# A projection in the place of a transposition at the crossing of the five-tile chunk, and four head groups per loop turn in a two-layer cross-attention kernel

## The chip, the cores and the metric

The kernel runs on one core of a Trainium2 chip. The metric is the device time of one execution in microseconds. All operands are float32 in memory. On TensorE the kernel multiplies in reduced formats, and it gets the accuracy back by splitting each operand into a high part and a low part (`_hi` and `_lo`), so that one exact product is made of three matmuls.

## The reference, cut to what matters

1024 query rows `x` of width 128 attend to 6404 context rows of width 128, with 16 heads of 64. A mixture-of-experts layer follows, then a second attention and a second mixture. In layer 0 queries and keys are RMS-normalized per head, and the 1024 latent rows are keys and values too:

```python
# layer 0 (xn, ln: layer norms of context and latents; rmsnorm per head of 64)
q = ln @ Wq;  kv = concat([xn @ Wkv, ln @ Wkv])        # 7428 keys
sim = (rmsnorm(q) * scale) @ rmsnorm(k).T
out = softmax(sim) @ v;  x = x + tanh(g) * (out @ Wout + bout)
# layer 1 (no norm of q and k, one extra null key and value): 6405 keys
out = softmax(scale * q @ k.T) @ v
x = x + tanh(g) * layernorm(out @ Wo)
```

## The kernel before, in words

**Groups, chunks, steps, pairs.** The 16 heads are worked off in 8 groups of 2 (`GH = 2`, `NG = 8`). The keys lie in tiles of 128: 59 in layer 0 and 51 in layer 1. `CHUNKS` cuts the tiles into ten chunks per layer. In layer 0 all chunks have 6 tiles, but for chunk 4, which has 5. A chunk is gone through twice: once for queries 0 to 511 (n = 0), then for queries 512 to 1023 (n = 1), the two query halves. A step is one tile of keys with one query half and both heads. A group has 118 steps in layer 0 and 102 in layer 1. The loops go by pairs of steps: pair i holds steps 2i and 2i+1. Chunk 4 of layer 0 is steps 48 to 57, so pairs 24 to 28. As it has an odd number of tiles, pair 26 holds its last step of the first half (52) and its first step of the second half (53). That is the crossing, `crossed` in the code.

**What an engine does in pair i.** TensorE (PE): the scores of steps 2i+2 and 2i+3 (`score`, line 1135, two `scores_ps` buffers in turn). Then, in odd pairs, `mix_last` (line 1143). Then the products of probabilities and values of steps 2i and 2i+1, from the high part (`mix_high`, line 1153) and the low part (`mix_low`, line 1160), which add up in `out_ps`. ScalarE (ACT): `exp` of steps 2i+2 and 2i+3 (line 659 in layer 0, two instructions for a step). VectorE (DVE): `p_low` of these steps (line 818: probabilities minus their high part), and after the last step of a half of a chunk `add_out` (lines 829, 831), which adds `out_ps` into `out_acc` and so frees `out_ps`. The first `mix_high` of the next half waits for it (`o_added`). At the crossing DVE's order is `p_low(54)`, `add_out` of step 52, `p_low(55)`.

**Items.** Keys and values of the next chunk are made two tiles at a time. Such an item k is a load and a turn. The load is `project_kv` on PE (line 1070, six matmuls into `proj_ps`), then on ACT `read_kv` (lines 628, 630, and the square of 634 in layer 0), then on DVE `v_low` (802, 804) and `k_var` (792, 795), and GpSimd (POOL) makes the reciprocal root (590). The turn is `transpose_k` on PE (1078, two transposes), then on ACT `k_high` (639) and `v_wide` (645), then on DVE `k_low` (810). There is one `proj_ps`, so `project_kv` of an item waits until `k_low` of the item before is done (`lo_done`), and `transpose_k` waits for `v_low` of its own item. Queries of the next group (`q_rows`, `q_cols`) and the output product (`final`) use `proj_ps` in between, at pairs that stay the same under the change. In pair 24 DVE also runs `bound_norm` (lines 871, 873, 881), between `p_low(51)` and that pair's items.

**Where an item stands.** `schedule(L)` (lines 166 to 205) writes the order by hand. It spreads the loads and turns of the next chunk evenly over the pairs of the present one, and puts each at the nearest slot: "s", "m" or "e". On PE "s" is ahead of the pair's products of values, "m" between them and "e" behind them. On ACT and DVE "s" is between the two steps of the pair, and "m" and "e" are both behind the second. So on ACT a load at "s" is read ahead of the pair's second `exp`. Every engine works strictly through its own list.

**The loop over groups.** On each engine `Fori(0, NG // 2)` holds the code of two groups (`g = two * 2 + odd`), so that a layer has four turns and three jumps back, behind groups 1, 3 and 5 (groups are counted from 0).

Of the kernel before, what the change touches and what calls it, by code (L numbers as in the profile page):

```python
# [40 lines left out]
GH = 2  # L41
NG = H // GH
CHUNKS = ((6, 6, 6, 6, 5, 6, 6, 6, 6, 6), (6, 6, 6, 5, 4, 4, 4, 4, 6, 6))
NB = 6
NPL = 4
VW = 36
# [119 lines left out]
def schedule(L):  # L166

    tiles = CHUNKS[L]
    first = [sum(tiles[:c]) for c in range(len(tiles))]
    steps = [(c, n, t) for c, m in enumerate(tiles) for n in range(2) for t in range(m)]  # L170
    item0 = [sum((m + 1) // 2 for m in tiles[:c]) for c in range(len(tiles) + 1)]
    slots = (("s", 0.2), ("m", 0.55), ("e", 1.0))
    turn, load = {}, {}
    for c, pairs in enumerate(tiles):
        n_items = (tiles[(c + 1) % len(tiles)] + 1) // 2
        for k in range(2 * n_items):
            at = (k + 1) * pairs / (2 * n_items)
            _, pair, slot = min((abs(p + x - at), p, s) for p in range(pairs) for s, x in slots)
            where = turn if k % 2 == 0 else load
            assert first[c] + pair not in where  # L180
            where[first[c] + pair] = (slot, item0[c + 1] + (k + 1) // 2)
    ends = {}
    for i, (c, n, t) in enumerate(steps):
        if t == tiles[c] - 1:
            ends.setdefault(i // 2, []).append((i, 2 * c + n))
    free = [p for p in sorted(load) if load[p][0] == "e" and turn.get(p - 1, " ")[0] == "e" and p - 1 not in ends]
    final = [p for p in free if p >= 5][:4]
    q_row = [p for p in free if p > final[-1]][:2]
    q_col = [p for p in free if p >= q_row[1] + 6][:2]
    events = {}  # L190
    for rank, slot in enumerate("sme"):
        for kind, table in (("turn", turn), ("load", load)):
            for pair, (at, k) in table.items():
                if at == slot:
                    events.setdefault(pair, []).append((rank, kind, k))
    return steps, item0, turn, load, {p: [("sme"[rank], kind, k) for rank, kind, k in sorted(e)] for p, e in events.items()}, ends, final, q_row, q_col


def attention_layer(nc, A, L, sem_, sb_, layer_norm, ln_stats, ln_apply, rstd, B):
# [6 lines left out]
    NT = REST + 1  # L206
    TL = CHUNKS[L]
    TM = max(TL) + max(TL) % 2
# [16 lines left out]
    with scope:  # L225
        def sb(name, shape, dt=F32, to=scope):
            return sb_("a%d_%s" % (L, name), shape, dt, to)
# [224 lines left out]
        vlast = sb("v_last", [P, 2, TM, GH, VW], F16)  # L452
        probs = sb("probs", [P, NB, NQ])
        plow = sb("probs_lo", [P, NPL, NQ], R32)
# [60 lines left out]
        def step_at(n2):  # L515
            return STEPS[n2 % NS] + (n2 % NS,)
# [12 lines left out]
        with nc.Block() as block:  # L529
            @block.sync  # L530
            def _(sp):
                def load_kv(r):
                    sp.dma_start(wkv_raw[:, :], A[NAME + "wkv_g"][bass.ds(r, 1), :, :].rearrange("a p n -> p (a n)")).then_inc(wkv_in, 16)

                def load_q(r):
                    sp.dma_start(wq_raw[:, :], A[NAME + "wq_g"][bass.ds(r, 1), :, :].rearrange("a p n -> p (a n)")).then_inc(wq_in, 16)

                def load_o(r):
                    sp.wait_ge(ql_done, 2 * r + 2)
                    sp.dma_start(wo_raw[:, :], A[NAME + "wo_g"][bass.ds(r, 1), :, :].rearrange("a p n -> p (a n)")).then_inc(wo_in, 16)  # L540
                    sp.dma_start(fin, A[NAME + "we_g"][bass.ds(r, 1), :, :].rearrange("a p n -> p (a n)")).then_inc(wo_in, 16)

                def load_den(r):
                    sp.wait_ge(o_added, 2 + r * NADD)
                    sp.dma_start(den_row.unsqueeze(0), oacc[P - 1:P, :, :]).then_inc(den_out, 16)
                    sp.wait_ge(den_out, 16 * (r + 1))
                    sp.dma_start(sums[:, 0, :], den_row.rearrange("h (p x) -> (h p) x", x=GH * NQ // P)).then_inc(sum_in, 16)
                    sp.wait_ge(den_rec, r + 1)
                    sp.dma_start(inv_row.rearrange("h (p x) -> (h p) x", x=GH * NQ // P), sums[:, 1, :]).then_inc(inv_out, 16)
                    sp.wait_ge(inv_out, 16 * (r + 1))  # L550
                    sp.wait_ge(c_ready, r + 1)
                    sp.dma_start(den[:, :, :], inv_row.partition_broadcast(P)).then_inc(den_in, 16)
                    sp.wait_ge(den_in, 16 * (r + 1))

                load_kv(0)
                load_q(0)
                with sp.Fori(0, NG // 2) as two:
                    for odd in range(2):
                        g = two * 2 + odd
                        load_o(g)  # L560
                        load_den(g)
                        sp.wait_ge(wkv_lo, g + 1)
                        load_kv(g + 1)
                        sp.wait_ge(wq_lo, g + 1)
                        load_q(g + 1)
                        if L == 1:
                            sp.wait_ge(v_ready, (g + 1) * NI)
                            r_ = CTX_REST
                            wide = [1, GH, P - 1]
                            sp.dma_start(v16[r_:r_ + 1, LASTP, T_LAST, :, 0:P - 1],  # L570
                                         null16[0:1, 0:P - 1].unsqueeze(1).broadcast_to(wide)).then_inc(null_in, 16)
                            sp.dma_start(v32[r_:r_ + 1, LASTP, T_LAST, :, 0:P - 1].bitcast(F32),
                                         null32[:, 0:P - 1].bitcast(F32).unsqueeze(1).broadcast_to(wide)).then_inc(null_in, 16)
                            for h in range(GH):
                                sp.dma_start(vlast[r_:r_ + 1, LASTP, T_LAST, h, 4:5], null16[0:1, P - 1:P]).then_inc(null_in, 16)
                load_o(NG)
                load_den(NG)

            @block.gpsimd
            def _(pool):  # L580
# [27 lines left out]
                bound(0)  # L608
                for k in range(2, HEAD + 1):
                    k_rstd(0, k)  # L610
                with pool.Fori(0, NG // 2) as two:
                    for odd in range(2):
                        g = two * 2 + odd
                        for i in range(NPR):
                            if i in LOAD:
                                k_rstd(g * NI, LOAD[i][1])
                            if i == Q_ROW[1] + 1:
                                q_root(g + 1)
                            if i == Q_ROW[1] + 6:
                                bound(g + 1)  # L620

            @block.scalar
            def _(act):
# [25 lines left out]
                def exp(s0, k0, n2):  # L649

                    c, n, t, idx = step_at(n2)
                    b, pb = n2 % 2, idx % NB
                    act.wait_ge(s_ready, s0 + n2 + 1)
# [93 lines left out]
                for n2 in range(2):  # L747
                    exp(0, 0, n2)
                read_kv(0, HEAD)
                with act.Fori(0, NG // 2) as two:  # L750
                    for odd in range(2):
                        g = two * 2 + odd
                        k0, s0 = g * NI, g * NS
                        for i in range(NPR):
                            if i == NPR - 1:
# [32 lines left out]
            def _(dve):  # L788
# [24 lines left out]
                def p_low(s0, n2):  # L813
                    idx = n2 % NS
                    dve.wait_ge(p_ready, s0 + n2 + 1)
                    if n2 >= NS:
                        dve.wait_ge(mixed, 2 * (s0 + n2) - 2)
                    nc.vector.tensor_tensor(plow[:, idx % NPL, :], probs[:, idx % NB, :], p_hi[:, idx % NB],  # L818
                                            ALU.subtract).then_inc(plo_ready, 1)
# [174 lines left out]
                    p_low(0, n2)  # L994
                v_low(0, HEAD)
                k_var(0, HEAD)
                with dve.Fori(0, NG // 2) as two:
                    for odd in range(2):
                        g = two * 2 + odd
                        k0, s0 = g * NI, g * NS  # L1000
                        for i in range(NPR):
                            p_low(s0, 2 * i + 2)
# [52 lines left out]
            def _(pe):  # L1055
# [83 lines left out]
                def mix_last(n1):  # L1139
                    c, n, t, idx = step_at(n1)  # L1140
                    for e in range(GH):
                        j = 32 * (2 * e + n1 % 2)
                        last = nc.tensor.matmul(last_ps[j:j + 32, :], vlast[:, c % 2, t, e, 4 - 4 * n:36 - 4 * n],  # L1143
                                                p_hi[:, idx % NB, e * 512:(e + 1) * 512],
                                                start=n1 < 2, stop=True, skip_group_check=True)
                    return last

                def mix_high(g, n1):
                    c, n, t, idx = step_at(n1)
                    for e in range(GH):  # L1150
                        if t == 0:
                            pe.wait_ge(o_added, g * NADD + 2 * (2 * c + n) + e + 1)
                        nc.tensor.matmul(outs[:, e * 512:(e + 1) * 512], v16[:, c % 2, t, e, :],  # L1153
                                         p_hi[:, idx % NB, e * 512:(e + 1) * 512], start=t == 0, stop=False)

# [23 lines left out]
                project_kv(0, HEAD, 0, QSIDE0 if HEAD == 2 else None)  # L1179
                for n2 in range(2):  # L1180
                    score(0, 0, 0, n2)
                with pe.Fori(0, NG // 2) as two:
                    for odd in range(2):
                        g = two * 2 + odd
                        k0, s0 = g * NI, g * NS

                        def item(i, slot):
# [321 lines left out]
```

## Time and profile before

| | us |
|---|---|
| median of 3 runs | 4484.49 (4479.59 to 4485.52) |
| the profiled execution, its own time | 4479.22 |
| span of the profile, first to last instruction | 4477.4 |
| PE busy, and its share of the span | 4194.4, 94% |
| DVE busy | 3394.0, 76% |
| ACT busy | 3191.6, 71% |
| POOL busy | 408.7, 9% |
| DMA traffic | 48.20 MB |
| mean granted TensorE clock | 0.974 of full speed |

The trace's times are counted from the start of the span. An engine's busy time is the union of its instructions. Waits, register operations and branches are not counted as busy. Where a text speaks of the start of a pair, it is the start of the first `scores_ps` matmul of that pair (line 1135); the windows below are cut at such starts, so their lengths are the lengths of pairs.

### The profile page before, as it was taken

What the parts mean: (1) busy time and instruction counts of PE and PEld (TensorE: products, weight loads), DVE (VectorE), ACT (ScalarE), POOL (GpSimd) and SP (SyncE); (2) the same over time, 40 slices, a digit from 0 to 9 for tenths busy, and PEclk for the clock granted to TensorE, in tenths of its full rate; (3) what the DMA queues carried; (4) which work ended last, traced back from release to release, by engine and by line L of the source; (5) the groups of instructions that cost most, each with busy time, mean ns of one, the idle gap of its engine ahead of it and who ended that gap; (6) DMA issues with size and microseconds to landing.
All of it is one profiled execution on the core that took longest, in us unless ns stands there. A gap on an engine that the chain in (4) does not pass through costs nothing. (4 is left out here: it accounts for less than half of the span.)

```text
span 4477.4 us, 76059 instructions
## 1 busy us (share of the span) xinstructions
PE 4194.4 (94%) x26651; PEld 2692.1 (60%) x26651; DVE 3394.0 (76%) x5328; ACT 3191.6 (71%) x5163; POOL 408.7 (9%) x348
## 2 busy tenths in 40 slices
PE   3999999999999999999978599999999999999995
PEld 2666666666666666666645366666666666666664
DVE  5878788787878888888742577777777777777775
ACT  3888888888888888888842367676766676766661
POOL 3111111111111111111100000000000000000000
PEclk9999999999999999999979699999999999999996
DMA  1000000000000000000011000000000000000000
GB/s 41 12 1 16 1 15 3 1 16 1 17 1 1 16 1 17 1 5 12 1 51 33 20 1 16 1 9 9 5 12 5 12 5 12 1 16 1 16 1 23
DMA packets 27290, 48.20 MB, mean 11 GB/s; under 512 B 9329, under 2 KB 18425, under 8 KB 24313
## 3 DMA queue, kind: packets, MB, share of 16 engines
q1 hardware_dynamic: 24824, 42.30, 2.9%
q8 instruction: 237, 3.88, 0.4%
q14 instruction: 163, 1.33, 0.1%
q10 hardware_dynamic: 2066, 0.69, 0.1%
HBM read 42.15 MB, written 0.82 MB: 10 GB/s over the span
## 5 line engine op out<-in xcount | busy, mean ns | idle before, releaser
L818 DVE TENSOR_TENSOR a_probs_lo<-a_probs 128x1024 fp32r<-128x1024 f32 x1764 | 2119.8, 1223 | 652.3 <-ACT a_probs L663 305.5
L659 ACT ACTIVATE a_probs<-scores_ps,a_c_bias,a_k_rstd 128x512 f32<-128x512 f32 x1892 | 1317.2, 776 | 35.3 <-PE scores_ps L1135 33.8
L1160 PE MATMUL out_ps<-a_probs_lo,a_v 128*128 128x512 f32 x3520 | 1134.5, 443 | 0.0
L1153 PE MATMUL out_ps<-a_probs,a_v 128*128 128x512 bf16 x3520 | 967.5, 390 | 38.1 <-DVE a_out_acc L831 27.8
L663 ACT ACTIVATE a_probs<-scores_ps,a_c_bias 128x1024 f32<-128x1024 f32 x818 | 870.3, 1112 | 114.5 <-PE scores_ps L1135 113.5
L1135 PE MATMUL scores_ps<-a_q_hi,a_k_hi 64*128 64x512 f32 x3528 | 793.0, 445 | 16.9 <-issue 9.1
L1160 PEld LDWEIGHTS out_ps<-a_probs_lo,a_v 128*128 128x128 f32 x3520 | 658.7, 188 | 219.9
L1135 PE MATMUL scores_ps<-a_q_lo,a_k_hi 64*128 64x512 f32 x3528 | 702.4, 393 | 0.0
L1135 PE MATMUL scores_ps<-a_q_hi,a_k_lo 64*128 64x512 f32 x3528 | 698.0, 390 | 0.0
L1153 PEld LDWEIGHTS out_ps<-a_probs,a_v 128*128 128x128 f16 x3520 | 273.5, 96 | 590.4 <-issue 221.9
L628 ACT ACTIVATE a_v<-proj_ps 128x256 f16<-128x256 f32 x456 | 175.5, 385 | 517.8 <-PE proj_ps L1070 517.6
L1135 PEld LDWEIGHTS scores_ps<-a_q_hi,a_k_hi 64*128 64x128 f32 x3528 | 332.8, 184 | 208.2 <-issue 107.9
L590 POOL TENSOR_TENSOR a_k_rstd<-a_k_stat,minus_half 128x4 f32<-128x4 f32 x244 | 301.9, 1237 | 1691.7 <-DVE a_k_stat L795 1691.7
L1135 PEld LDWEIGHTS scores_ps<-a_q_lo,a_k_hi 64*128 64x128 f32 x3528 | 335.1, 185 | 76.1
L831 DVE TENSOR_TENSOR a_out_acc<-out_ps,a_out_acc 128x512 f32<-128x512 f32 x576 | 369.2, 682 | 11.4 <-PE out_ps L1160 11.4
L1135 PEld LDWEIGHTS scores_ps<-a_q_hi,a_k_lo 64*128 64x128 f32 x3528 | 335.0, 186 | 37.6
L639 ACT ACTIVATE a_k_hi<-proj_ps 128x256 fp32r<-128x256 f32 x454 | 175.3, 386 | 248.4 <-PE proj_ps L1078 247.9
L645 ACT ACTIVATE a_v<-a_v 128x512 fp32r<-128x512 f16 x454 | 284.0, 626 | 0.0
L1143 PE MATMUL spare_ps<-a_probs,a_v_last 128*32 128x512 bf16 x3520 | 282.7, 395 | 0.0
L1070 PE MATMUL proj_ps<-a_wkv_hi,a_x_hi 128*128 128x256 f32 x912 | 267.5, 293 | 13.8 <-ACT normed_T L696 6.4
L1070 PE MATMUL proj_ps<-a_wkv_lo,a_x_hi 128*128 128x256 f32 x912 | 259.0, 284 | 0.0
L1070 PE MATMUL proj_ps<-a_wkv_hi,a_x_lo 128*128 128x256 f32 x912 | 257.1, 282 | 0.0
(194 smaller groups left out, 3404.9 us busy)
## 6 DMA issues: line engine op xcount, KB each, us to landing
a_den<-a_inv_row SPq DMA_DIRECT2D x18, 1024.0 KB, 4.7
normed<-in_L_xattn_we_g SPq DMA_DIRECT2D x18, 256.0 KB, 2.7
a_wkv_raw<-in_L_xattn_wkv_g SPq DMA_DIRECT2D x18, 128.0 KB, 2.1
a_wo_raw<-in_L_xattn_wo_g SPq DMA_DIRECT2D x18, 128.0 KB, 2.1
m_w<-in_L_ffn_w1T SPq DMA_DIRECT2D x1, 2048.0 KB, 8.4
m_w<-in_L_ffn_w2T SPq DMA_DIRECT2D x1, 2048.0 KB, 12.8
a_wq_raw<-in_L_xattn_wq_g SPq DMA_DIRECT2D x18, 64.0 KB, 1.9
residual<-in_x SPq DMA_DIRECT2D x1, 512.0 KB, 4.0
```

The source lines that it names most:

```text
L590: nc.gpsimd.tensor_tensor(krs[:, par, 2 * j:2 * j + 2, :].rearrange("p t h -> p (t h)"), kst[:, 1, :], mhalf[:, 0:2 * GH], ALU.pow).then_i ...
L628: nc.scalar.activation(v16[:, par, 2 * j:2 * j + 2, :, 0:DH].rearrange("p t h d -> p (t h) d"), proj[:, 2 * P:4 * P].rearrange("p (a d) -> ...
L645: nc.scalar.activation(v32[:, par, 2 * j:2 * j + 2, :, :].rearrange("p t h k -> p (t h) k"), v16[:, par, 2 * j:2 * j + 2, :, :].rearrange( ...
L659: ins = nc.scalar.activation(probs[:, pb, e * 512:(e + 1) * 512], scores[:, b, e * 512:(e + 1) * 512], ACT.Exp, bias=cbias[:, tile:tile + ...
L663: ins = nc.scalar.activation(probs[:, pb, :], scores[:, b, :], ACT.Exp, bias=cbias[:, 1:2] if last else cbias[:, 0:1])
L818: nc.vector.tensor_tensor(plow[:, idx % NPL, :], probs[:, idx % NB, :], p_hi[:, idx % NB], ALU.subtract).then_inc(plo_ready, 1)
L831: ins = nc.vector.tensor_tensor(oacc[:, e, q], outs[:, e * 512:(e + 1) * 512], oacc[:, e, q], ALU.add)
L1070: last = nc.tensor.matmul(dst, a[:, x], w[:, :].rearrange("p (a c) -> p a c", a=2), start=t == 0 and m == 0, stop=m == 2, skip_group_check ...
L1135: last = nc.tensor.matmul(scores[:, b, e * 512:(e + 1) * 512], kk[r, c % 2, t, :], qq[r, n * 512:(n + 1) * 512], start=m == 0, stop=m == 2)
L1143: last = nc.tensor.matmul(last_ps[j:j + 32, :], vlast[:, c % 2, t, e, 4 - 4 * n:36 - 4 * n], p_hi[:, idx % NB, e * 512:(e + 1) * 512], sta ...
L1153: nc.tensor.matmul(outs[:, e * 512:(e + 1) * 512], v16[:, c % 2, t, e, :], p_hi[:, idx % NB, e * 512:(e + 1) * 512], start=t == 0, stop=False)
L1160: nc.tensor.matmul(outs[:, e * 512:(e + 1) * 512], v32[:, c % 2, t, e, :], plow[:, idx % NPL, e * 512:(e + 1) * 512], start=False, stop=t ...
```

## The change

Two things. `schedule` no longer spreads the three items evenly in a chunk of five pairs whose next chunk has six tiles. It takes places from `AMID`. Only chunk 4 of layer 0 meets the condition. Layer 1 keeps its order. The places of loads (K) and turns (T) of items 15 to 18 become:

| pair | before | after |
|---|---|---|
| 24 | T15 at e | T15 at m |
| 25 | K16 at m | K16 at s, T16 at e |
| 26 (crossing) | T16 at m | K17 at m |
| 27 | K17 at s | T17 at m |
| 28 | T17 at s, K18 at e | K18 at e |
| 29 | T18 at e | T18 at e |

And the loops over groups hold four groups instead of two, on all five engines, so that a layer has two turns and one jump back, behind group 3.

```diff
+AMID = (0.55, 1.2, 2.0, 2.55, 3.55, 5.0)
...
             at = (k + 1) * pairs / (2 * n_items)
+            if pairs == 5 and n_items == 3:
+                at = AMID[k]
             _, pair, slot = min((abs(p + x - at), p, s) for p in range(pairs) for s, x in slots)
...
-                with pe.Fori(0, NG // 2) as two:
-                    for odd in range(2):
-                        g = two * 2 + odd
+                with pe.Fori(0, NG // 4) as four:
+                    for sub in range(4):
+                        g = four * 4 + sub
```

The last hunk stands five times, once for each of `sp`, `pool`, `act`, `dve` and `pe`.

## Rows read from the trace of the kernel before

**Rows 1.** The page, busy time by engine (share of the span):
```profile
PE 4194.4 (94%) x26651; PEld 2692.1 (60%) x26651; DVE 3394.0 (76%) x5328; ACT 3191.6 (71%) x5163; POOL 408.7 (9%) x348
```
**Rows 2.** Windows, pairs 24 to 29, layer 0, group 1 (stretch: length, busy, PEclk, DMA):
```profile
492.72:497.17 4.45, 3.98 (x24) 2.38 (x23) 4.42 (x9) 3.75 (x7) 0.97 (x1) 1.00 0.02 6
497.17:502.26 5.09, 5.07 (x35) 2.85 (x34) 4.92 (x8) 4.47 (x9) 0.97 (x1) 1.00 0.00 0
502.26:508.04 5.78, 4.11 (x25) 2.32 (x24) 4.57 (x9) 3.87 (x7) 1.01 (x1) 1.00 0.00 0
508.04:512.94 4.90, 4.90 (x37) 3.00 (x36) 2.85 (x7) 3.16 (x7) 0.37 (x1) 1.00 0.00 0
512.94:517.94 5.00, 4.83 (x30) 3.05 (x29) 3.20 (x5) 4.29 (x8) 0.11 (x1) 1.00 0.00 0
517.94:522.27 4.33, 4.33 (x32) 2.50 (x31) 4.30 (x9) 3.76 (x7) 3.59 (x3) 1.00 0.02 4
```
**Rows 3.** Windows: pairs 31 and 36 (layer 0), pair 36 (layer 1):
```profile
527.59:531.90 4.31, 4.31 (x32) 2.51 (x32) 2.65 (x6) 3.76 (x7) 1.01 (x1) 1.00 0.00 0
550.38:554.60 4.22, 4.22 (x27) 2.94 (x26) 3.11 (x6) 3.69 (x6) 0.00 (x0) 1.00 0.00 0
2941.20:2945.76 4.56, 4.56 (x29) 3.17 (x28) 2.42 (x6) 2.86 (x5) 0.00 (x0) 1.00 0.00 0
```
**Rows 4.** Windows: pair 27, layer 0, groups 3 and 4 (PEclk is third from last):
```profile
1048.70:1055.11 6.41, 6.41 (x36) 3.74 (x35) 2.85 (x7) 3.16 (x7) 0.37 (x1) 0.73 0.00 0
1321.80:1328.20 6.40, 6.40 (x35) 3.74 (x35) 2.85 (x7) 3.15 (x7) 0.37 (x1) 0.73 0.01 3
```
**Rows 5.** Windows: last pair of groups 0, 1, 5 (both layers) through next pair 5:
```profile
376.46:408.92 32.46, 31.65 (x203) 20.10 (x202) 28.41 (x42) 28.98 (x52) 4.90 (x3) 1.00 0.16 53
645.39:680.60 35.21, 32.51 (x204) 19.85 (x204) 28.49 (x42) 29.09 (x52) 3.96 (x3) 1.00 0.17 51
1729.69:1764.62 34.93, 32.33 (x203) 19.95 (x203) 28.38 (x42) 29.07 (x52) 3.95 (x3) 1.00 0.15 50
2773.70:2805.65 31.95, 31.47 (x203) 20.18 (x202) 26.22 (x37) 23.63 (x34) 0.00 (x0) 1.00 0.17 53
3002.33:3035.26 32.93, 31.27 (x204) 20.14 (x203) 26.33 (x37) 23.41 (x34) 0.00 (x0) 1.00 0.16 53
3918.83:3951.70 32.87, 31.26 (x204) 20.17 (x204) 26.41 (x37) 23.41 (x34) 0.00 (x0) 1.00 0.17 54
```
**Rows 6.** Timeline behind group 1 (start, us, engine, instruction, idle before and its releaser):
```profile
651.37 0.50 PE L1135 MATMUL scores_ps<-a_q_hi,a_k_hi 64*128 64x512 f32 x2 [1.35 <-issue]
653.77 1.45 ACT L659 ACTIVATE a_probs<-scores_ps,a_c_bias,a_k_rstd 128x512 f32<-128x512 f32 x2 [2.61 <-PE scores_ps L1135]
656.25 1.23 DVE L818 TENSOR_TENSOR a_probs_lo<-a_probs 128x1024 fp32r<-128x1024 f32 x1 [2.88 <-issue]
```
**Rows 7.** Timeline of pair 25, group 1:
```profile
498.33 1.21 DVE L871 TENSOR_REDUCE a_q_stat<-a_den 128x16 f32<-128x1024 f32 x1
...
499.33 0.56 PEld L1153 LDWEIGHTS out_ps<-a_probs,a_v 128*128 128x128 f16 x4 [0.45 <-issue]
500.43 0.19 PEld L1070 LDWEIGHTS proj_ps<-a_wkv_hi,a_x_hi 128*128 128x128 f32 x1 [0.54 <-DVE a_k_lo L810]
```
**Rows 8.** Timeline of pair 26, group 1:
```profile
504.75 1.23 DVE L818 TENSOR_TENSOR a_probs_lo<-a_probs 128x1024 fp32r<-128x1024 f32 x1 [1.18 <-ACT a_probs L659]
...
506.64 0.40 PE L1153 MATMUL out_ps<-a_probs,a_v 128*128 128x512 bf16 x1 [1.47 <-DVE a_out_acc L831]
```
**Rows 9.** Timeline of pairs 27 and 28, group 1:
```profile
510.19 0.38 PE L1070 MATMUL proj_ps<-a_wkv_hi,a_x_hi 128*128 128x256 f32 x1
...
512.21 1.43 ACT L659 ACTIVATE a_probs<-scores_ps,a_c_bias,a_k_rstd 128x512 f32<-128x512 f32 x2
513.94 1.45 ACT L659 ACTIVATE a_probs<-scores_ps,a_c_bias,a_k_rstd 128x512 f32<-128x512 f32 x2 [0.29 <-PE scores_ps L1135]
...
516.07 1.46 ACT L659 ACTIVATE a_probs<-scores_ps,a_c_bias,a_k_rstd 128x512 f32<-128x512 f32 x2
```

More of the change, by code:

```diff
@@ L556, in _ @@
                 load_q(0)
-                with sp.Fori(0, NG // 2) as two:
-                    for odd in range(2):
-                        g = two * 2 + odd
+                with sp.Fori(0, NG // 4) as four:
+                    for sub in range(4):
+                        g = four * 4 + sub
                         load_o(g)
@@ L610, in _ @@
                     k_rstd(0, k)
-                with pool.Fori(0, NG // 2) as two:
-                    for odd in range(2):
-                        g = two * 2 + odd
+                with pool.Fori(0, NG // 4) as four:
+                    for sub in range(4):
+                        g = four * 4 + sub
                         for i in range(NPR):
@@ L749, in _ @@
                 read_kv(0, HEAD)
-                with act.Fori(0, NG // 2) as two:
-                    for odd in range(2):
-                        g = two * 2 + odd
+                with act.Fori(0, NG // 4) as four:
+                    for sub in range(4):
+                        g = four * 4 + sub
                         k0, s0 = g * NI, g * NS
@@ L996, in _ @@
                 k_var(0, HEAD)
-                with dve.Fori(0, NG // 2) as two:
-                    for odd in range(2):
-                        g = two * 2 + odd
+                with dve.Fori(0, NG // 4) as four:
+                    for sub in range(4):
+                        g = four * 4 + sub
                         k0, s0 = g * NI, g * NS
@@ L1181, in _ @@
                     score(0, 0, 0, n2)
-                with pe.Fori(0, NG // 2) as two:
-                    for odd in range(2):
-                        g = two * 2 + odd
+                with pe.Fori(0, NG // 4) as four:
+                    for sub in range(4):
+                        g = four * 4 + sub
                         k0, s0 = g * NI, g * NS
```

## The prediction

> **What bounds the kernel now.** I read the page's busy times first. PE is busy for 94% of the span, DVE for 76% and ACT for 71% [rows 1]. So PE is the bound on the whole, and what it loses it loses in short waits at certain pairs. These I looked for by cutting windows at the starts of the pairs. The reader is to see in them the length of a pair beside PE's busy time. Pairs 31 and 36, which hold the same work as many others, are all PE: 4.31 of 4.31 us for an odd pair with a turn (it has `mix_last` too), 4.22 of 4.22 for an even one with a load [rows 3]. In the chunk that the change touches, pair 24 has 0.47 us without PE, pair 26 has 1.67, pair 28 has 0.17 [rows 2]. Then I took the timeline of pair 26. PE stands for 1.47 us before the first `mix_high` of step 53 and is let go by `add_out` (L831) [rows 8]. The addition doesn't wait for PE. It waits behind `p_low(54)`, which started at 504.75 after 1.18 us of waiting for ACT's `exp` of step 54. So the crossing ends by ACT's chain and not by what PE does meanwhile. Last I looked at the borders between groups, which are the same code with and without a jump back behind them.
>
> **The loop.** I compare the stretch from a group's last pair through pair 5 of the next group, without a jump and with one. Layer 0: 32.46 us behind group 0, 35.21 behind group 1, 34.93 behind group 5. Layer 1: 31.95, 32.93, 32.87 [rows 5]. The jumps behind groups 1 and 5 fall away, the one behind group 3 stays, and the borders that lose their jump get the code that groups 0 and 1 have between them now. That is (35.21 - 32.46) + (34.93 - 32.46) = 5.2 us in layer 0 and (32.93 - 31.95) + (32.87 - 31.95) = 1.9 us in layer 1, together 7.1 us. Where it goes can be seen behind group 1: PE stands 1.35 us on issue, ACT's next `exp` comes after 2.61 us of idle time, DVE's next `p_low` after 2.88 us on issue [rows 6]. In layer 0 ACT and DVE are then late and cost PE more in the pairs behind; in layer 1, with its lighter ACT, this is mostly made up. Bounds: nothing, if the longer code costs the same waits at other places, and 7.1. I take 7.1: the jumps cost alike, and a border without one has only 0.81 us without PE in its stretch (32.46 less 31.65), against 2.70 with one [rows 5], though its code is fetched too. The stretches hold what SP's and POOL's jumps cost as well.
>
> The Trainium skill has two rules on this. "Advanced Engine Details and Errata", section "Control Flow Timing", gives some 108 ns for a compare-and-branch. By that figure four removed jumps would be worth about 0.4 us, an estimate. "Runtime: NRT & Kernel Launch", section "Instruction fetch mechanics", says that a taken branch to a page that is not at hand stalls until a DMA has fetched it, while straight code is fetched ahead. The 2.6 to 2.9 us of ACT and DVE agree with the second rule and not with the first [rows 6].
>
> **The order in chunk 4, walked through with group 1's times.** The change moves items; no engine gets an instruction more or less, and no DMA moves.
>
> Pair 24: the transposes of item 15 come a little earlier on PE, with the same work to the end. `k_low(15)` on DVE keeps its place behind `bound_norm`. I leave the pair at 4.45.
>
> Pair 25: K16 goes from "m" to "s", ahead of the products of values. They begin at 499.33 now, and K16 at 500.43, let go by `k_low(15)` (L810), which stands behind `bound_norm`, whose L871 begins at 498.33 and takes 1.21 [rows 7]. DVE's list ahead of it is unchanged, so K16 starts at 500.43 again, only that now PE has nothing to do from 499.33 on: a new wait of 1.10 us. Behind it stand the pair's eight products of values, which were half done by then. A load at "s" and the eight products take from 510.19 to 512.94 in pair 27, so 2.75 us [rows 9, 2]. T16 is added, at 4.56 - 4.22 = 0.34 [rows 3]. Pair 26 begins at 500.43 + 2.75 + 0.34 = 503.52 in place of 502.26. Pair 25 is 6.35 long, not 5.09.
>
> Pair 26: what counts is `exp(54)`. On ACT `exp(53)` now stands behind `read_kv(16)`. In pair 27 a load at "s" starts at 510.19 and the second `exp` at 512.21, 2.02 later [rows 9]. So `exp(53)` starts at 502.45. Then come `k_high(16)`, `v_wide(16)` and `exp(54)`; in pair 28 `exp`, the same two and the next `exp` start 516.07 - 513.94 = 2.13 apart [rows 9]. `exp(54)` starts at 504.58, ends 1.45 later at 506.03, and `p_low(54)` starts 0.03 behind, at 506.06. It was 504.75 [rows 8], so the crossing is late by 1.31, and pair 27 starts at 509.35 and not 508.04. The first `mix_high` of step 53 then starts at 506.64 + 1.31 = 507.95. K17 is hidden ahead of it: PE had done its part of the pair, transposes too, at 506.64 - 1.47 = 505.17, which is 2.91 behind the pair's start, so it would be there at 506.43 now; the load could take 1.5 us more than the transposes and still not be late. Pair 26 is 5.83 long.
>
> Pair 27 holds a turn at "m" in place of a load at "s" and becomes like pair 31, 4.31 (4.90 before). Pair 28 keeps its load and loses the turn, and becomes like pair 36, 4.22 (5.00 before) [rows 2, 3]. Pair 29 then starts at 509.35 + 4.31 + 4.22 = 517.88, against 517.94. The gain is 0.06 us in a group and 0.5 us in eight. What the change gives at the crossing and behind it, it takes in pair 25. Bounds of this term: if pairs 27 and 28 stay as long as they are, 1.31 us worse in a group, 10.5 in all; if K16 at "s" had not to wait, the rival below, 1.0 better in a group. My value lies between, where the rows of the same lists put it.
>
> **The clock.** In groups 3 and 4 pair 27 took 6.41 and 6.40 us against 4.90 in group 1, at a granted clock of 0.73, a mean over a stretch partly at 2.4 and partly at 1.2 GHz. In both it is the pair behind the 1.47 us wait [rows 4, 2, 8]. That is 3.0 us. After the change the wait in pair 25 is 1.10, and the one in pair 26 is 507.95 - 506.43 = 1.52 less what a load takes more than two transposes, which is not measured apart; in any case six matmuls are more than two transposes (0.34), so I count some 1 us, and both waits shorter than the 1.47 of before. PE's wait of 1.35 behind a jump in layer 0 went without a fall [rows 6, 5]. So I expect both falls to go: 3.0 us. Bounds: a fall at every wait, below, and 3.0.
>
> **The sum.** 7.1 + 0.5 + 3.0 = 10.6 us off the profiled execution, whose own time was 4479.2 (span 4477.4 and 1.8 around it), so 4468.6. That execution stands 5.3 under the median of the three runs. Nothing in it says why the others were longer, so I take the difference off the median: 4484.5 - 10.6 = 4473.9, rounded 4474. A difference of 0.2% is 9 us; less than that I call the same.
>
> **The rivals.**
> The crossing is filled and nothing new waits (0.20): K16 finds `k_low(15)` done, pair 25 costs only T16 more (5.09 + 0.34), pair 26 stays 5.78, pairs 27 and 28 shrink. Pairs 24 to 28 are 4.45 + 5.43 + 5.78 + 4.31 + 4.22 = 24.19 long, against 25.22 now [rows 2]. That is 1.03 us in a group and 8.2 in eight, with 7.1 and 3.0 together 18.3: 4466. For it: ACT and DVE both have slack on the whole. Against it: the release by L810 at 500.43 [rows 7].
> The clock falls twice as before (0.15): 7.6 us, 4477. For it: two waits of over 1 us follow within 8 us.
> Pairs 27 and 28 do not shrink (0.08): 1.31 a group, so 7.1 + 3.0 - 10.5 = -0.4, 4485. For it: ACT arrives at pair 27 late by 1.3. Against it: in pair 27 ACT is busy for only 3.16 of 4.90 and DVE for 2.85 [rows 2].
> The loop brings nothing (0.06): a body twice as long costs at the jump that stays, or at new places, what the others saved: 3.5 us, 4481. Against it: the jumps' costs don't depend on what went before.
> Slower (0.06): the clock falls at both waits of the chunk in every group. One fall costs 1.5, sixteen cost 24, less 10.6: +13.4, 4498. It decides from 14 falls on ((9 + 10.6) / 1.5 = 13.1). For it: the two known falls follow the longest wait of the chunk. Against it: that wait stands in all eight groups and the clock fell behind it in two.
>
> **How the numbers follow.** The forecast has 0.45; its own values spread by some 4 us either way, of which about 0.7 lies more than 9 us under the median. Faster: 0.45 x 0.7 + 0.20 + a little of the second rival, 0.54. Slower 0.06, the same 0.40. The range goes from 4463, the filled crossing with a little over, to 4486, the rival in which pairs 27 and 28 don't shrink; what is outside is the slower rival and the tail below.
>
> **What would show it.** The loop: behind groups 1 and 5 no idle time on issue of 1.35 on PE and 2.9 on DVE, and stretches of 32.5 and 31.95; one jump behind group 3 with 35.1 and 33.0. Chunk 4: pair 25 about 6.3, with PE let go by L810 before L1070; pair 26 about 5.8, pair 27 4.3, pair 28 4.2, and 24 to 29 together 29.5 as before. The clock: pair 27 of like length in all groups. I am wrong in the walk if pair 25 is near 5.4, and in the clock if any pair of chunk 4 differs among groups by 1.5.

## The result, and the profile after

The changed kernel takes 4470.66 us (median of 10 runs, 4469.06 to 4473.44), the one before 4482.32 (10 runs, 4479.59 to 4485.96). The ratio is 0.9973, with an interval from 0.9964 to 0.9982: faster by 11.7 us, where 10.6 were forecast. The interval goes from 8 to 16 us: the sign is clear, but the bar that the prediction set between "the same" and "faster" (0.2%, 9 us) lies inside it. The profiled execution took 4470.64 (before 4479.22).

First the windows of pairs 24 to 29, layer 0, group 1, to be laid beside [rows 2]. The columns are the same: the stretch, its length, busy time of PE, PEld, DVE, ACT and POOL, the granted clock, DMA.

```profile
493.86:498.30 4.44, 3.99 (x25) 2.28 (x24) 4.41 (x9) 4.30 (x9) 0.98 (x1) 1.00 0.03 6
498.30:504.52 6.22, 5.10 (x37) 3.31 (x37) 5.21 (x11) 3.62 (x8) 1.06 (x2) 1.00 0.00 0
504.52:510.46 5.94, 4.58 (x27) 2.87 (x26) 4.84 (x6) 4.93 (x10) 0.90 (x1) 1.00 0.00 0
510.46:514.77 4.31, 4.14 (x31) 2.44 (x31) 2.92 (x7) 3.31 (x6) 0.37 (x1) 1.00 0.02 4
514.77:519.00 4.23, 4.23 (x28) 2.99 (x27) 2.70 (x4) 3.06 (x5) 0.00 (x0) 1.00 0.00 0
519.00:523.33 4.33, 4.16 (x30) 2.51 (x30) 4.30 (x9) 3.76 (x7) 3.32 (x3) 1.00 0.00 0
```

Their sum is 29.47, against 29.55. Pair 25 grew by 1.13 us, pair 26 by 0.16, and pairs 27 and 28 gave back 0.59 and 0.77. The other seven groups show the same lengths within 0.04. PE's busy time is a little too small in this trace, since it lacks 440 matmul records (26211 against 26651 weight loads).

The timeline of the same group shows how the chain runs (start, us, engine, line, instruction, idle before and its releaser; the lines stand three further on than before, so L813 is `k_low`, L662 `exp`, L821 `p_low`, L834 `add_out`, L1073 `project_kv`):

```profile
501.09 0.41 DVE L813 TENSOR_TENSOR a_k_lo<-proj_ps,a_k_hi 128x256 fp32r<-128x256 f32 x1
...
501.55 0.19 PEld L1073 LDWEIGHTS proj_ps<-a_wkv_hi,a_x_hi 128*128 128x128 f32 x1 [1.55 <-DVE a_k_lo L813]
...
503.58 1.43 ACT L662 ACTIVATE a_probs<-scores_ps,a_c_bias,a_k_rstd 128x512 f32<-128x512 f32 x2
...
505.69 2.79 ACT L662 ACTIVATE a_probs<-scores_ps,a_c_bias,a_k_rstd 128x512 f32<-128x512 f32 x4
...
507.18 1.22 DVE L821 TENSOR_TENSOR a_probs_lo<-a_probs 128x1024 fp32r<-128x1024 f32 x1 [0.57 <-ACT a_probs L662]
508.33 1.28 DVE L834 TENSOR_TENSOR a_out_acc<-out_ps,a_out_acc 128x512 f32<-128x512 f32 x2
...
509.07 0.40 PE L1156 MATMUL out_ps<-a_probs,a_v 128*128 128x512 bf16 x1 [1.16 <-DVE a_out_acc L834]
```

K16 waits for `k_low(15)`, which stands behind `bound_norm`. `exp(53)` follows K16 by 2.03, `exp(54)` by 2.11 more, `p_low(54)` by 1.49, the first product of step 53 by 1.89. From K16 to the start of pair 27 it is 8.91 us; the walk had 8.92.

The borders between groups, from the last pair through pair 5, beside [rows 5]: layer 0 behind groups 1 and 3, layer 1 behind groups 1 and 3.

```profile
646.49:678.96 32.47, 30.95 (x200) 20.17 (x203) 28.43 (x42) 28.97 (x52) 4.90 (x3) 1.00 0.16 52
1184.22:1219.19 34.97, 31.61 (x202) 19.92 (x204) 28.22 (x42) 29.08 (x52) 3.96 (x3) 1.00 0.16 50
2993.79:3025.75 31.96, 30.74 (x201) 20.17 (x203) 26.23 (x37) 23.63 (x34) 0.00 (x0) 1.00 0.16 53
3451.02:3483.70 32.68, 30.76 (x202) 20.14 (x204) 26.38 (x37) 23.39 (x34) 0.00 (x0) 1.00 0.17 54
```

Behind groups 1 and 5 the stretches are as long as those that never had a jump. Behind group 3 the one jump is left.

The page counts the DMA queues that bring instructions (packets, MB, share). First the kernel before, then the changed one:

```profile
q8 instruction: 237, 3.88, 0.4%
q14 instruction: 163, 1.33, 0.1%
```
```profile
q8 instruction: 229, 3.75, 0.3%
q14 instruction: 145, 1.19, 0.1%
```

With four jumps fewer in the two layers together, 0.27 MB of instructions less are fetched.

### The profile page after: what moved, and what is told of

It is laid out like the page before. It is cut to its first block and busy times, and to the rows that moved or that the text cites. A ratio compares the mean times of both kernels' runs of the same rounds, so it can differ in the third digit from the quotient of the medians.

```text
span 4468.7 us, 75551 instructions
## 1 busy us (share of the span) xinstructions
PE 4112.0 (92%) x26211; PEld 2695.0 (60%) x26651; DVE 3395.1 (76%) x5328; ACT 3190.0 (71%) x5163; POOL 410.6 (9%) x348
## 5 line engine op out<-in xcount | busy, mean ns | idle before, releaser
L821 DVE TENSOR_TENSOR a_probs_lo<-a_probs 128x1024 fp32r<-128x1024 f32 x1764 | 2120.7, 1223 | 641.0 <-ACT a_probs L666 303.5
L662 ACT ACTIVATE a_probs<-scores_ps,a_c_bias,a_k_rstd 128x512 f32<-128x512 f32 x1892 | 1316.3, 776 | 31.7 <-PE scores_ps L1138 30.2
L1156 PE MATMUL out_ps<-a_probs,a_v 128*128 128x512 bf16 x3080 | 857.7, 389 | 112.0 <-issue 51.2
L834 DVE TENSOR_TENSOR a_out_acc<-out_ps,a_out_acc 128x512 f32<-128x512 f32 x576 | 369.4, 683 | 11.4 <-PE out_ps L1163 11.4
L1073 PE MATMUL proj_ps<-a_wkv_hi,a_x_hi 128*128 128x256 f32 x912 | 265.3, 291 | 21.3 <-DVE a_k_lo L813 12.6
L1073 PE MATMUL proj_ps<-a_wkv_lo,a_x_hi 128*128 128x256 f32 x912 | 259.0, 284 | 0.0
L1073 PE MATMUL proj_ps<-a_wkv_hi,a_x_lo 128*128 128x256 f32 x912 | 257.0, 282 | 0.0
```

The costliest lines, as they stand in the source:

```text
L662: ins = nc.scalar.activation(probs[:, pb, e * 512:(e + 1) * 512], scores[:, b, e * 512:(e + 1) * 512], ACT.Exp, bias=cbias[:, tile:tile + ...
L834: ins = nc.vector.tensor_tensor(oacc[:, e, q], outs[:, e * 512:(e + 1) * 512], oacc[:, e, q], ALU.add)
L1073: last = nc.tensor.matmul(dst, a[:, x], w[:, :].rearrange("p (a c) -> p a c", a=2), start=t == 0 and m == 0, stop=m == 2, skip_group_check ...
```

## The experiments

The kernel before ran beside each set of experiments, and each ratio, with its interval, is to the kernel before of its own set. Its medians there were 4482.86 (new order alone, four groups alone, `bound_norm` moved, `add_out` first), 4483.94 (eight groups, one group, `add_out` first in the kernel before, all edits), 4481.99 (`bound_norm` moved in the kernel before, old order with all edits) and 4481.19 (the last run). Differences of medians within 2 us are not read. Differences to the changed kernel go across sets: taken by way of the kernel before of each set instead, they come out larger by 0.5 to 1.6 us.

**The two parts apart.** The new order with two groups in a turn:

```diff
-                with pe.Fori(0, NG // 4) as four:
-                    for sub in range(4):
+                with pe.Fori(0, NG // 2) as turn:      # on all five engines
+                    for sub in range(2):
```

> The new order of chunk 4 alone, two groups in a turn as before. My theory: pairs 24 to 29 of layer 0 become what they are in the changed kernel (4.45, 6.21, 5.94, 4.31, 4.22, 4.32, sum 29.45 against 29.55), which is 0.1 us in a group and 0.8 in all; the two falls of the clock behind the old 1.47 us wait do not come, 3.0 us in the profiled run. So 1 us of the difference in a run without falls before, 4 in the profiled one; the jumps behind groups 1, 3, 5 stay with 35.2 and 33.0. Rival, the order is the whole gain: 11 us less than before.

4478.55, ratio 0.9991 (0.9982 to 1.0000), so 4.3 us less than before, with an interval from nothing to 8. Pairs 24 to 29 sum to 29.41 to 29.47 in all groups, as in the changed kernel, and the clock falls in no pair of chunk 4. It fell once in layer 1, behind the jump of group 3 (the stretch takes 34.67 against 33.37 behind group 1; the granted clock is the third number from the end):

```profile
2997.19:3030.56 33.37, 31.27 (x203) 20.14 (x203) 26.41 (x37) 23.41 (x34) 0.00 (x0) 1.00 0.17 53
3455.87:3490.54 34.67, 32.82 (x204) 20.90 (x203) 26.49 (x37) 23.73 (x34) 0.00 (x0) 0.95 0.16 51
```

At this jump PE had stood for 1.85 us, and the clock fell 0.5 us after it went on:

```profile
3462.37 0.50 PE L1138 MATMUL scores_ps<-a_q_hi,a_k_hi 64*128 64x512 f32 x2 [1.85 <-issue]
```

The old order with four groups in a turn (the loop lines of the change alone):

> Four groups in a turn alone, the old order of chunk 4. My theory: stretches behind groups 1 and 5 fall to 32.5 and 31.95, 7.1 us less than before; pair 26 has its 1.47 us wait in all groups, and the clock still falls behind it in some groups (pair 27 at 6.4 in 0 to 4 of 8), so the remainder to the changed kernel is 1 to 6 us. Rival, the falls of the clock have nothing to do with the order but with where the run begins: the clock falls in as few groups of chunk 4 here as in the changed kernel, and the remainder is under 1 us.

4474.64, ratio 0.9982 (0.9973 to 0.9991), so 8.2 less (4 to 12 by the interval). The borders behind groups 1 and 5 are as in the changed kernel. In one group of eight the clock fell at pair 27:

```profile
1045.90:1052.30 6.40, 6.40 (x35) 3.73 (x35) 2.85 (x7) 3.16 (x7) 0.37 (x1) 0.73 0.00 0
```

8.2 and 4.3 are 12.5, against 11.7 for both together: the parts add up within what the medians tell. The rival that the order is the whole gain falls. One fall of the clock doesn't decide the rival about the falls; it is counted over all traces below.

**More and fewer jumps.** The changed kernel with `NG // 8`, eight groups in one turn:

> The changed kernel with all eight groups in one turn: no jump back at all. My theory, a jump costs what the stretches behind it show: the one that is left behind group 3 costs 34.96 - 32.47 = 2.5 in layer 0 and 32.67 - 31.96 = 0.7 in layer 1, so 3.2 us less than the changed kernel, and no other stretch changes. Rival, the cost is of fetching code as such and moves: the stretch behind group 3 falls but other pairs grow, and the time stays within 1 us.

4467.79, ratio 0.9965 (0.9952 to 0.9979), 2.9 less than the changed kernel; 3.2 were expected. The borders behind group 3 in layer 0 and in layer 1 now read

```profile
1184.12:1216.59 32.47, 30.93 (x202) 20.11 (x204) 28.37 (x42) 28.99 (x52) 4.83 (x3) 1.00 0.17 52
3447.17:3479.16 31.99, 30.70 (x200) 20.16 (x202) 26.23 (x37) 23.62 (x34) 0.00 (x0) 1.00 0.16 53
```

and no other border grew by more than 0.1. This run changes one thing more than the jump: with a single turn the register arithmetic of the loops is gone too (the trace has 66885 instructions in place of 75551), and pair 25 of layer 0 fell from 6.2 to 6.1 us in every group. So the 2.9 us are not of the jump alone. The kernel before with `Fori(0, NG)`, one group in a turn:

> The kernel before with one group in a turn: seven jumps in a layer instead of three. My theory, jumps add up: four more in each layer at 2.6 and 0.95 us, 14 us more than before, and as each jump is a wait of PE of 1.35 us in layer 0 and more in layer 1, some falls of the clock besides (1.5 each), so 14 to 20 more. Rival, the length of the body matters (a shorter body is fetched sooner): a jump costs under 1.5 us in layer 0, less than 8 us more in all.

4499.52, ratio 1.0042 (1.0028 to 1.0056), 15.6 more than before. Three borders follow: behind group 0 in layer 0 and in layer 1, both with a new jump, and behind group 1 in layer 1, where the kernel before has a jump too; there the clock fell:

```profile
377.05:412.17 35.12, 31.75 (x200) 19.88 (x204) 28.38 (x42) 29.05 (x52) 3.95 (x3) 1.00 0.16 50
2779.04:2812.00 32.96, 30.58 (x199) 20.16 (x202) 26.41 (x37) 23.39 (x34) 0.00 (x0) 1.00 0.17 53
3008.64:3043.60 34.96, 31.99 (x201) 20.83 (x204) 26.46 (x37) 23.71 (x34) 0.00 (x0) 0.95 0.16 50
```

Over all traces a jump lengthens the border by 2.5 to 2.7 us in layer 0 (23 jumps). In layer 1 it is 0.7 to 1.6 us (18 jumps without a fall of the clock; 2.7 to 3.0 in the five with one), so the 0.7 to 1.1 that the traces of before and after show is too narrow. The costs of bodies of one, two and four groups overlap (layer 1: 0.8 to 1.1, 0.9 to 1.6 and 0.7 to 1.4), so no effect of the body's length shows.

**The wait that the new order made.** The changed kernel with `bound_norm` moved:

```diff
-                                if i == Q_ROW[1] + 5:
+                                if i == Q_ROW[1] + 8:
                                     bound_norm(g + 1)      # layer 0; GpSimd's bound(g + 1) from + 6 to + 9
```

> The changed kernel with bound_norm of layer 0 on DVE moved from pair 24 to pair 27 (and GpSimd's bound from pair 25 to 28). My theory: k_low(15) is ready 1.4 us earlier, K16 at s in pair 25 starts at once, 1.1 us earlier; pair 25 is 5.1 and not 6.2, pair 26 stays 5.9 since all its chain starts with K16, pairs 27 to 29 stay; 1.1 us in a group, 8.9 us less than the changed kernel. Rival, ACT holds pair 26: exp(54) cannot come earlier, so pair 26 grows by what pair 25 loses and the time stays within 1 us.

4462.19, ratio 0.9955 (0.9941 to 0.9968), 8.5 less than the changed kernel. In group 1, pairs 25 and 26, and the start of K16:

```profile
496.85:501.99 5.14, 5.14 (x39) 3.28 (x38) 3.83 (x8) 3.64 (x8) 1.10 (x2) 1.00 0.00 0
501.99:507.90 5.91, 4.57 (x27) 2.88 (x26) 4.83 (x6) 4.91 (x10) 0.88 (x1) 1.00 0.00 0
```
```profile
498.00 0.41 DVE L813 TENSOR_TENSOR a_k_lo<-proj_ps,a_k_hi 128x256 fp32r<-128x256 f32 x1
499.00 0.19 PEld L1073 LDWEIGHTS proj_ps<-a_wkv_hi,a_x_hi 128*128 128x128 f32 x1 [0.45 <-issue]
```

`k_low(15)` is done 0.6 us ahead of K16, pair 25 lost its 1.08 us and pair 26 kept its length, since its whole chain hangs on K16. The same edit in the kernel before:

> The kernel before (old order, two groups in a turn) with bound_norm of layer 0 moved from pair 24 to pair 27. My theory: in the old order K16 stands at m in pair 25 and waited for k_low(15) only 0.2 to 0.3 us; pair 25 becomes 4.8, pair 26 stays 5.77 with its 1.47 us wait, 2 us less than before in all (the same edit gave the changed kernel 8.5). So the wait of 1.1 us is made by the new order, and was not there before it. Rival: bound_norm held the whole stretch in the old order too, and the gain is 6 us or more.

4485.25, ratio 1.0008 (0.9999 to 1.0017): no gain, where 2 us were expected. Pair 25 did fall, from 5.09 to 4.81. But pair 28 grew from 5.00 to 6.04, which I had not seen coming, so that pairs 24 to 29 take 0.76 us more in a group. In the old order T17 stands at "s" and K18 at "e" of pair 28, and `k_low(17)` between them now has `bound_norm` (L871 to L881) and a late `p_low(58)` ahead of it:

```profile
515.96 1.21 DVE L871 TENSOR_REDUCE a_q_stat<-a_den 128x16 f32<-128x1024 f32 x1
...
517.61 1.23 DVE L818 TENSOR_TENSOR a_probs_lo<-a_probs 128x1024 fp32r<-128x1024 f32 x1
518.76 0.42 DVE L810 TENSOR_TENSOR a_k_lo<-proj_ps,a_k_hi 128x256 fp32r<-128x256 f32 x1
```
```profile
519.23 0.19 PEld L1070 LDWEIGHTS proj_ps<-a_wkv_hi,a_x_hi 128*128 128x128 f32 x1 [1.67 <-DVE a_k_lo L810]
```

What this run was for it did show: in the old order `bound_norm` cost pair 25 only 0.28 us, in the new one 1.08.

**The crossing.** The changed kernel with `add_out` of the crossing ahead of `p_low(54)`:

```diff
+                            crossed = i in ENDS and ENDS[i][0][0] % 2 == 0
+                            if crossed:
+                                add_out(g, s0, *ENDS[i][0])
                             p_low(s0, 2 * i + 2)
                             items(g, i, "s")
...
-                            crossed = i in ENDS and ENDS[i][0][0] % 2 == 0
-                            if crossed:
-                                add_out(g, s0, *ENDS[i][0])
                             p_low(s0, 2 * i + 3)
```

> The changed kernel with add_out of step 52 ahead of p_low(54) on DVE at the crossing (in layer 1 too, pair 20). My theory: add_out waits only for mix_low(52), and starts about 507.25 in place of 508.33 in group 1; the first mix_high of step 53 follows at about 508.0 in place of 509.07; pair 26 is about 4.85 and not 5.94, pair 27 stays 4.3 because p_low(54) and (55) are still done 1.5 us ahead of their use; 8.7 us less than the changed kernel. Rival: p_low(54) and p_low(55), later by 1.3, hold mix_low(54) in pair 27, and pair 27 gives back half or more: 0 to 4 us less.

4454.93, ratio 0.9940 (0.9926 to 0.9954), 15.7 less than the changed kernel where 8.7 were expected. Pairs 26 and 27 of layer 0, and the additions with PE's products:

```profile
503.33:507.96 4.63, 4.43 (x28) 2.87 (x27) 3.70 (x5) 4.60 (x10) 0.89 (x1) 1.00 0.00 0
507.96:512.28 4.32, 4.32 (x32) 2.43 (x31) 4.03 (x8) 3.64 (x7) 0.37 (x1) 1.00 0.02 4
```
```profile
505.82 1.29 DVE L834 TENSOR_TENSOR a_out_acc<-out_ps,a_out_acc 128x512 f32<-128x512 f32 x2 [0.42 <-PE out_ps L1163]
...
506.56 0.40 PE L1156 MATMUL out_ps<-a_probs,a_v 128*128 128x512 bf16 x1
```

The addition is now let go by PE itself, PE goes from K17 into the products without a stop, and pair 26 lost 1.31 us. I had forgotten to count layer 1, whose crossing (pair 20) fell from 5.43 to 4.63 in every group: 8 x (1.31 + 0.80) = 16.9. The same edit in the kernel before:

> The kernel before (old order, two groups in a turn) with add_out of step 52 ahead of p_low(54) at the crossing, in layer 1 too. My theory: in group 1 mix_low(52) is done near 504.9, so add_out starts at 505.0 in place of 505.90; pair 26 is 4.7 to 4.9 and not 5.77, pair 27 stays 4.9 or grows a little by k_low(16), pair 20 of layer 1 falls from 5.43 to 4.63 as in the changed kernel; 1.0 + 0.8 us in a group, 14 us less than before, and no fall of the clock at pair 27. Rival: the old order gains less from it, since the transposes have less work to hide than the projection: pair 26 stays above 5.3, under 10 us less.

4461.16, ratio 0.9952 (0.9938 to 0.9966), 22.8 less than before. Pair 26 fell from 5.77 to 4.63, pair 20 of layer 1 to 4.63, pair 27 stayed 4.91 in all groups: 8 x (1.14 + 0.80) = 15.5 by the lengths of pairs. The two profiled executions are 16.8 us apart, and that closes: 15.5, plus 3.0 for the two falls before, less 1.5 for a fall behind a jump of layer 1 that this execution had. The other 6 us lie between the medians and the profiled executions (the kernel before: 4483.94 against 4479.22; this one: 4461.16 against 4462.43), and no trace shows where they come from.

**All together, and what the order is worth then.**

> The changed kernel with the three other edits together: bound_norm at pair 27, add_out ahead of p_low(54), eight groups in one turn. My theory, they add up, since each takes away a wait of its own: 8.5 + 15.7 + 3.2 = 27 us less than the changed kernel, 4443 to 4444. Pairs 24 to 29 of layer 0 sum to 27.1. Rival: with add_out first, ACT's chain in pair 26 no longer sets the crossing, or another wait comes up behind bound_norm in pair 27 or 28, and one of the gains is lost: 4450 or more.

4443.94 (4443.34 to 4444.42), ratio 0.9912 (0.9896 to 0.9927), 26.7 less than the changed kernel, where 27 were expected. It beats both kernels. Pairs 25 to 28:

```profile
495.81:500.92 5.11, 5.03 (x37) 3.27 (x37) 3.79 (x8) 3.63 (x8) 1.03 (x2) 1.00 0.01 3
500.92:505.55 4.63, 4.43 (x29) 2.88 (x28) 3.71 (x5) 4.60 (x10) 0.90 (x1) 1.00 0.00 0
505.55:509.86 4.31, 4.14 (x30) 2.40 (x30) 4.03 (x8) 3.64 (x7) 1.01 (x1) 1.00 0.01 2
509.86:514.09 4.23, 4.23 (x29) 2.99 (x28) 4.08 (x7) 3.05 (x5) 0.00 (x0) 1.00 0.02 4
```

The old order with the same three edits, and then without the move of `bound_norm`:

> The old order with the three other edits of the 4443.9 us kernel (bound_norm at pair 27, add_out first, eight groups in a turn). It says what the new order is worth when both its waits are gone. My theory: pairs 24 to 29 are 4.4 + 4.8 + 4.6 + 4.9 + 5.0 + 4.3 = 28.1 and not 27.0, because K17 at s in pair 27 and T17 with K18 in pair 28 stay; 1.1 us in a group, 8.8 us more, 4452 to 4453. Rival: with add_out first the crossing has no wait to hide anything in, the order no longer matters, and the time is within 2 us of 4444.

> The old order with add_out first and eight groups in a turn, bound_norm back at pair 24 where that order wants it. The new order with the same two edits and bound_norm at pair 27 took 4443.9, the old order with bound_norm at pair 27 took 4459.2. My theory: moving bound_norm hurt the old order (k_low(17) stood behind it in pair 28, 1 us a group) and helps only where its old place holds a load; here pairs 24 to 29 are 4.4 + 5.1 + 4.6 + 4.9 + 5.0 + 4.3 = 28.4, 0.6 a group less than with the move, so 4454 to 4455, and the new order at its best is worth 1.4 us a group, 11 us. Rival: the 5.92 us of pair 28 comes from add_out first and eight groups and not from bound_norm's place: 4459 again.

4459.21 (ratio 0.9949, 0.9935 to 0.9962) and 4452.27 (ratio 0.9936, 0.9923 to 0.9950). The first was expected at 4452 to 4453 and is off by 7, for the reason just seen, which its expectation did not yet know of: its pair 28 is 5.92. With `bound_norm` back it is 5.01, and pair 25 4.96:

```profile
496.61:501.57 4.96, 4.79 (x35) 2.85 (x36) 4.89 (x8) 4.48 (x9) 0.91 (x1) 1.00 0.01 3
```

So each order with the better of the two tried places of `bound_norm`: 4443.9 against 4452.3. The new order is worth 8.4 us by the medians (11.1 by way of the kernel before of each set) and 9.9 by the lengths of pairs 24 to 29 (28.26 against 27.02), once the two waits on DVE that it meets are gone. It was expected at 11: the old order's pair 25 came out at 4.96 and not 5.1. In the change as made it was worth 0.08 us in a group.

## Why the prediction was right

**The loop, 7.1 us.** Right. The two borders lost 35.21 - 32.47 and 34.93 - 32.47 in layer 0, and 32.93 - 31.96 and 32.87 - 31.95 in layer 1, 7.1 together. The jump that stays behind group 3 was 0.13 cheaper in layer 0 and 0.34 in layer 1. The loop alone gave 8.2 in the medians, and the runs with one, two and four groups in a turn show that jumps add up. That the cost is of fetching code was argued. The instruction queues agree: 5.21 MB with three jumps in a layer, 4.94 with one, 5.46 with seven. What an engine waits for while it stands on issue no trace names.

**Chunk 4, 0.5 us.** Right, and by its own steps. Pair 25 was forecast at 6.35 and is 6.22, pair 26 5.83 and 5.94, pair 27 4.31 and 4.31, pair 28 4.22 and 4.23. The 0.13 in pair 25 is that K16, eight products and T16 took 2.97 and not 3.09; pair 26 has nearly as much more, since the chain from K16 to its end is 8.91 us, as walked. The cause of the new wait was argued from one releaser, `k_low` behind `bound_norm`; moving `bound_norm` took it away.

**The clock, 3.0 us.** For the profiled execution the size was right: groups 3 and 4 now take 4.30 and 4.32 at pair 27, not 6.41 and 6.40. But 3.0 is the count of one execution. The four traces with the old order and the old crossing have 2, 1, 0 and 1 such falls, 4 in 32 passes. The nine traces of the other kernels have none in 72 passes. Of these, 32 passes have the crossing's wait shortened to some 1.16 us, and 40 have no wait there. None in the first 32 against 4 in 32 could still be chance, so it isn't shown that a wait shorter by 0.3 us is what spares the fall. And I had bound the falls to that wait alone. There were five falls behind jumps in layer 1, in 23 such jumps, and none in 23 in layer 0. Behind the five PE had stood 1.8 to 2.2 us; none followed the 11 jumps of layer 1 with less than 1.8 us. But seven jumps of layer 1 with 1.8 to 2.3 us went without a fall, and so did all 23 of layer 0 with 1.0 to 1.7 us, some of them longer than the wait at the crossing. So the length of one wait doesn't decide it. The loop change takes away chances for a fall too.

**The sum.** Between the two profiled executions there are 8.6 us and not 10.6. Besides the 7.5, 0.6 and 3.0 of the three terms, pair 0 of group 0 took 6.56 against 5.02, since the clock rose 3.7 us later after the first pairs (0.7 came back in pair 3), and the tail from the last pair on took 102.46 against 100.49, at a granted clock of 0.60 against 0.62. Both are outside the changed code and go with a lower clock. That leaves 8.3 of the 8.6. The medians are further apart, by 11.7. The profiled execution of before lies below all ten of its runs, that of the changed kernel at its median, and no trace shows what the slower runs before had. So that 11.7 comes so near to 10.6 is in part luck: the interval is 8 us wide. The forecast of 4474 is 3.3 us above the measured 4470.7, of which 2.2 are that the median of three runs (4484.49) lay above that of ten (4482.32). The runs also differ less where fewer long waits are left: 6.4 us between the ends before and 4.4 after, in ten runs each, 1.1 in four runs of the kernel with all edits. Falls of the clock would fit that, but it isn't shown.

**The chances.** That K16 finds `k_low(15)` done had 0.20, and in the change as made it doesn't. It is what the kernel with `bound_norm` moved does: 4462 there, 4466 forecast for the rival. The slower side did not come near.

## What to carry to other kernels

Work that is put into a wait must itself be ready: ask what releases it, and what stands ahead of that on its own engine's list. Here the gap at the crossing was not PE's to fill; its release stood behind an instruction on DVE that waited for something else, and turning those two around was worth more than the whole change. And an edit that helps one order can hurt another, so after a move the neighbours' best places have to be looked for again.

## What the runs showed of the hardware

A jump back cost 2.5 to 2.7 us of the tightly coupled loop of layer 0 and 0.7 to 1.6 us in layer 1, whether the body held one, two or four groups, and the same code without the jump cost nothing that the stretches show. The engines do not pay it at one time: behind group 1 PE stood 1.35 us on issue and DVE 2.88 [rows 6]. The Trainium skill says in "Runtime: NRT & Kernel Launch", section "Instruction fetch mechanics", that a taken branch breaks the sequential fetching ahead. The queues that fetch instructions agree, with 5.21 MB before and 4.94 after.

The granted clock fell from 2.4 to 1.2 GHz behind 4 of 32 waits of PE of 1.47 us at the old crossing, and behind 5 of 23 jumps of layer 1, where PE had stood 1.8 to 2.2 us. Behind the jumps of layer 0, with 1.0 to 1.7 us, it fell in none of 23. Each fall cost some 1.5 us more. So a wait that costs its own length in each pass can cost 1.5 us more in some, and which passes these are, the length of the wait doesn't tell.
